# Rows of x turned between product tiles, and two low quarters on VectorE, in a graph + attention + expert layer on one core

## The chip, the cores and the metric

One core of a Trainium2 chip runs the whole layer as one program of 25298 instructions. The metric is the device time of one execution in microseconds. Before the change three runs gave 1471.56, 1474.73 and 1475.39 us, median 1474.73 us.

## What is computed

The reference takes x (1250 rows of 1024), 20000 edges (src, dst) sorted by dst, and the weights of three sublayers. Cut to what matters here:

```python
xn = layernorm(x)
# graph sublayer: count matrix of the edges (+ identity), degrees, then
h   = xn @ W.T + b
out = segment_sum(deg_inv_sqrt[row] * deg_inv_sqrt[col] * h[col], row)
x = x + graph(xn) + attention_with_random_features(xn)
x = x + top2_of_8_experts(layernorm(x))
```

The change touches only the first part: turning xn, the product `xn @ W.T`, and the edge count matrix.

## The kernel before

Rows are padded to 1280 and cut in TT = 10 blocks of 128. Three things are made in the first 290 us.

1. xn. ScalarE and GpSimd normalise the ten row blocks. TensorE transposes each block in two halves of four 128x128 pieces (L1633; index i = 0 to 19, block t = i // 2) into a PSUM bank. ScalarE copies the bank, rounded, to `xh` (L935), VectorE subtracts that from the bank and writes the rest to `xl` (L1199). The banks are 3 to 6 in turn. This is one loop on each engine, and TensorE then waits for all twenty halves (`xt_low` at 2 * TT) ahead of the first product tile.

2. The count matrix, in ten graph blocks of 128 rows. For each block VectorE makes one-hot matrices of its edges: a 128x128 one (L1192) and a 128x1280 one (L1193), called one one-hot below; there are 188 in all, in a ring of four buffers. TensorE multiplies each pair in three matmuls (L1616) into banks 0 to 2 (even blocks) or 3 to 5 (odd blocks), between an opening (L1609, L1611) and a closing (L1621). ScalarE's `keep_block(b)` squares what was left of the block before (L910), then copies the banks twice (L922, L923). GpSimd's `degrees(b)` adds the copy to the degrees (L689), makes the rests of it (L691) and stores them by a DMA from its own queue (L693). Blocks 0 to 9 need 52, 24, 20, 16, 16, 12, 12, 12, 12 and 12 one-hots.

3. The product h, in 40 tiles (i = TT * q + t) of 24 matmuls, by four quarters of the weight columns. For each of a quarter's eight slabs ScalarE rounds a raw slab to `wqh` (L906, `high_quarter`), and the rest of it goes to `wql` (L683, `low_quarter`). There are four raw buffers; SyncE loads the next slab when `w_ready` says that the low part of the slab four back was made. A tile ends in bank 6 or 7 and ScalarE copies it out (L956); TensorE may be at most two tiles ahead of that.

Each engine works strictly in its written order. TensorE does graph block 0, the twenty turns, and then tiles 0 to 39 with graph blocks 1 to 9 put in before tiles 3, 7, 10, 14, 17, 21, 24, 28 and 31 (`BREAKS`). ScalarE follows the same order, with `high_quarter(1)` right behind the turns and `high_quarter(2)` and `(3)` ahead of the copy of tiles 11 and 22. VectorE does one_hots(0), the twenty lows, then one_hots(1) to (9), as far ahead as the four buffers allow. GpSimd does low_quarter(0), degrees(0), low_quarter(1), degrees(1), (2), low_quarter(2), degrees(3) to (5), low_quarter(3), degrees(6) to (9). The graph product, the attention, the output projection and the experts follow; they hang on these results and are untouched.

Of the kernel before, what the change touches and what calls it, by code (L numbers as in the profile page):

```python
# [8 lines left out]
P = 128  # L9
N, D = 1250, 1024  # L10
TT = -(-N // P)
NP = TT * P
LAST = N - (TT - 1) * P
KT = D // P
# [24 lines left out]
BREAKS = (3, 7, 10, 14, 17, 21, 24, 28, 31)  # L39
DEG_AT = 33  # L40
REST_AT = 35

RING = 6
START = 5
# [3 lines left out]
ALU = mybir.AluOpType  # L48
# [11 lines left out]
def gps_layer(nc, x, dst_pairs, src_cols, dst_cols, wg, bg, wq, bq, wk, bk, wv, bv, wo, bo, orf,  # L60
# [6 lines left out]
    with ctx:  # L67
# [131 lines left out]

        def counts(b):  # L200
            return ATf[:, b + 1, :] if b < TT - 1 else last_raw

        def xn_tile(t):
            return xn_low[:, t, :] if t < TT // 2 else xn_high[:, t - TT // 2, :]
# [75 lines left out]
        def bank(b, n=CW):  # L280
            return PB[:, 512 * b:512 * b + n]
# [348 lines left out]
        def _(pool):  # L630
# [48 lines left out]
            def low_quarter(q):  # L679
                for k in range(KT):  # L680
                    i = KT * q + k
                    pool.wait_ge(w_high, i + 1)
                    g.tensor_tensor(wql[q % 2][:, k, :], raw_g[:, i % 4, :], wqh[q % 2][:, k, :].bitcast(F32),  # L683
                                    ALU.subtract).then_inc(w_ready, 1)

            def degrees(b):
                pool.wait_ge(at_evac, b + 3)
                pool.wait_ge(s_pchain, b + 1)
                g.tensor_tensor(degacc[:, :], degacc[:, :], counts(b), ALU.add).then_inc(s_pchain, 1)  # L689
                pool.wait_ge(s_pchain, b + 2)  # L690
                g.tensor_tensor(counts(b).bitcast(F32R), counts(b), AT[:, b, :].bitcast(F32), ALU.subtract).then_inc(rest_made, 1)  # L691
                pool.wait_ge(rest_made, b + 1)
                g.dma_start(rests[b], counts(b).bitcast(F32R)).then_inc(rest_stored, 16)  # L693
                if b == 0:
                    g.dma_start(rests[TT][:, 0:P], counts(0)[:, 0:P].bitcast(F32R)).then_inc(rest_stored, 16)
# [3 lines left out]
            low_quarter(1)  # L699
            for b in range(1, 3):  # L700
                degrees(b)
            low_quarter(2)
            for b in range(3, 6):
                degrees(b)
            low_quarter(3)
            for b in range(6, TT):
                degrees(b)
            pool.wait_ge(s_degcol, TT)
            g.tensor_tensor(dis[:, :], deg[:, :], mhalf[:, :], ALU.pow).then_inc(s_dis, 1)
# [177 lines left out]
        def _(act):  # L887
# [12 lines left out]
            def high_quarter(q):  # L900
                for k in range(KT):
                    i = KT * q + k
                    act.wait_ge(raw_in[i % 4], 16 * (i // 4 + 1))
                    if q >= 2:
                        act.wait_ge(tile_done, TT * (q - 1))
                    a.activation(wqh[q % 2][:, k, :], raw_g[:, i % 4, :], ACT.Copy).then_inc(w_high, 1)  # L906
# [5 lines left out]
            def keep_block(b):  # L912
                act.wait_ge(at_done, b + 1)
                if b >= 1:
                    rest_squares(b - 1)
                    act.wait_ge(rest_sum, b)
                    act.wait_ge(rest_stored, 16 * (b + 1))
                if b == TT - 2:

                    act.wait_ge(w_ready, NQ * KT)  # L920
                of = PB[:, 1536 * (b % 2):1536 * (b % 2) + NP]
                a.activation(AT[:, b, :], of, ACT.Copy)  # L922
                a.activation(counts(b), of, ACT.Copy).then_inc(at_evac, 1)  # L923

            def high_scaled(q):
                for b in range(TT):
                    act.wait_ge(h_bias, TT * max(q - 1, 0) + b + 1)
                    a.mul(hh[:, q % 2, b, :], hrf[:, q % 2, b, :], dis[:, b:b + 1]).then_inc(h_hi, 1)

            high_quarter(0)  # L930
            keep_block(0)
            for i in range(2 * TT):
                t, k0 = i // 2, 4 * (i % 2)
                act.wait_ge(xt_done, i + 1)
                a.activation(xh[:, k0:k0 + 4, t * P:(t + 1) * P],  # L935
                             bank(3 + i % 4).rearrange("p (k n) -> p k n", k=4), ACT.Copy).then_inc(xt_high, 1)
            high_quarter(1)
            for i in range(TILES):
                q, t = i // TT, i % TT
                if i in BREAKS:  # L940
                    keep_block(BREAKS.index(i) + 1)
                if i in (11, 22):
                    high_quarter(2 + i // 22)
                if i == REST_AT:
                    rest_squares(TT - 1)
                if i == TILES - 1:
                    act.wait_ge(s_dis, 1)
                    high_scaled(0)
                act.wait_ge(tile_done, i + 1)
                if i < SPILL:  # L950
                    to = hrf[:, q, t, :]
                else:
                    to = spill[:, i % 2, :]
                    if i >= SPILL + 2:
                        act.wait_ge(h_stored[i % 2], 16 * ((i - SPILL) // 2))
                a.activation(to, bank(7 - i % 2, QW), ACT.Copy).then_inc(tile_evac, 1)  # L956
# [181 lines left out]
        def _(dve):  # L1138
# [44 lines left out]
            def one_hots(b):  # L1183
                first = dve.value_load(rngi[0:1, 0, b:b + 1], min_val=0, max_val=PAIRS - 2)
                count = dve.value_load(rngi[0:1, 1, b:b + 1], min_val=1, max_val=PAIRS // 2)
                begin = dve.value_load(rngi[0:1, 3, b:b + 1], min_val=0, max_val=PAIRS * TT)
                with dve.Fori(0, count) as i:
                    at = nc.s_assert_within(first + 2 * i, 0, PAIRS - 2, skip_runtime_bounds_check_because="the last pair that a block needs is below PAIRS - 1")
                    for p in range(4):
                        col = 2 * at + p  # L1190
                        dve.wait_ge(oh_free, 4 * (begin + i) + p + 1)
                        v.tensor_scalar(ohd[:, p, :], iota[:, b * P:(b + 1) * P], dc[:, ds(col, 1)], None, ALU.is_equal)  # L1192
                        v.tensor_scalar(ohs[:, p, :], iota[:, :], sc[:, ds(col, 1)], None, ALU.is_equal).then_inc(oh_ready, 1)  # L1193

            one_hots(0)
            for i in range(2 * TT):
                t, k0 = i // 2, 4 * (i % 2)
                dve.wait_ge(xt_high, i + 1)
                v.tensor_tensor(xl[:, k0:k0 + 4, t * P:(t + 1) * P], bank(3 + i % 4).rearrange("p (k n) -> p k n", k=4),  # L1199
                                xh[:, k0:k0 + 4, t * P:(t + 1) * P].bitcast(F32), ALU.subtract).then_inc(xt_low, 1)  # L1200
            for b in range(1, TT):
                one_hots(b)

            def low_scaled(q, b):
                dve.wait_ge(h_hi, TT * q + b + 1)
# [388 lines left out]
        def _(pe):  # L1594
# [7 lines left out]
            def graph_block(b):  # L1602
# [19 lines left out]
                             start=False, stop=True, skip_group_check=True)  # L1622
                ins.then_inc(at_done, 1)

            graph_block(0)
            for i in range(2 * TT):
                t = i // 2
                pe.wait_ge(s_xn, t + 1)
                if i >= 4:
                    pe.wait_ge(xt_low, i - 3)  # L1630
                for q in range(4):
                    k = 4 * (i % 2) + q
                    ins = nc.tensor.transpose(bank(3 + i % 4)[:, q * P:(q + 1) * P], xn_tile(t)[:, k * P:(k + 1) * P], ident[:, :])  # L1633
                ins.then_inc(xt_done, 1)
            pe.wait_ge(xt_low, 2 * TT)
            for i in range(TILES):
                q, t = i // TT, i % TT
                if i in BREAKS:
                    graph_block(BREAKS.index(i) + 1)
                if i == DEG_AT:  # L1640
                    pe.wait_ge(s_pchain, TT + 1)
                    pe.wait_ge(at_evac, TT + 1)
                    for c0, n in CHUNKS:
                        ins = mm(PB[:, c0:c0 + n], ones[:, :], degacc[:, c0:c0 + n], start=True, stop=True)
                    ins.then_inc(s_deg, 1)
                if i == REST_AT + 1:
                    pe.wait_ge(rest_sum, TT)
                    mm(bank(3, TT)[0:1, :], ones[:, 0:1], lsum[:, :], start=True, stop=True).then_inc(s_deg, 1)
                if i >= 2:
                    pe.wait_ge(tile_evac, i - 1)  # L1650
                for k in range(KT):
                    pe.wait_ge(w_ready, KT * q + k + 1)
                    at = slice(t * P, (t + 1) * P)
                    o = bank(7 - i % 2, QW)
                    mm(o, xh[:, k, at], wqh[q % 2][:, k, :], start=(k == 0), stop=False)  # L1655
                    mm(o, xh[:, k, at], wql[q % 2][:, k, :], start=False, stop=False)  # L1656
                    ins = mm(o, xl[:, k, at], wqh[q % 2][:, k, :], start=False, stop=(k == KT - 1))  # L1657
                ins.then_inc(tile_done, 1)
# [341 lines left out]
```

## Time and profile before

| | us |
|---|---|
| median of three runs | 1474.73 |
| the profiled execution, its own time | 1479.25 |
| its span, first to last instruction | 1477.70 |
| TensorE busy in the span | 1367.7 |
| VectorE busy | 789.1 |
| ScalarE busy | 561.8 |
| GpSimd busy | 428.5 |

All rows below are of one profiled execution. In a timeline a row is: start in us, length in us, engine, source line, operation, output<-inputs, shapes, count, and in brackets the idle time of the engine before it with what ended it. Lines that follow each other may be merged in a row with a count above one; the length is then that of the group. PE is TensorE, PEld its weight load, DVE VectorE, ACT ScalarE, POOL GpSimd. A chain row is start, length, and the piece of work or the wait on the path that ended last.

### The profile page before, as it was taken

How to read it: one execution, taken by the hardware profiler on the slowest of the kernel's cores; microseconds unless marked ns; L12 is line 12 of the kernel's file. 1: busy time of each engine (PE TensorE's matmuls, PEld its weight loads, DVE VectorE, ACT ScalarE, POOL GpSimd, SP SyncE). 2: the span in 40 equal slices, each digit the busy share in tenths (PEclk: the TensorE clock that was granted, in tenths of full speed). 3: DMA queues.
4: the chain of work that ended last, by engine and by line, in shares of the span. 5: the costliest groups of instructions: out<-in, count | busy, mean ns of one | idle time of the engine just before them, and what ended most of it. 6: DMA issues, size and time to landing. Idle time of an engine off the chain costs nothing.

```text
span 1477.7 us, 25298 instructions
## 1 busy us (share of the span) xinstructions
PE 1367.7 (93%) x8199; PEld 1206.9 (82%) x8234; DVE 789.1 (53%) x1633; ACT 561.8 (38%) x957; POOL 428.5 (29%) x429
## 2 busy tenths in 40 slices
PE   5799989999999999999999999979999399999996
PEld 1476667999989999999999999967888387778785
DVE  7856554436256565656565656564454634444541
ACT  7422222402045454545454545421222223444441
POOL 7432453253420101010101010045032533333332
PEclk9999999999989999999999999968999599999998
DMA  4110111264310000000000000013245356766843
GB/s 164 49 46 24 60 65 61 78 195 137 97 44 15 29 14 28 14 28 14 28 14 28 14 28 0 0 57 101 73 174 190 119 173 202 208 205 213 285 128 55
DMA packets 58101, 127.78 MB, mean 86 GB/s; under 512 B 7626, under 2 KB 28826, under 8 KB 58048
## 3 DMA queue, kind: packets, MB, share of 16 engines
q1 hardware_dynamic: 48016, 96.79, 19.0%
q0 software_dynamic: 10032, 30.30, 8.6%
q8 instruction: 31, 0.51, 0.1%
q14 instruction: 22, 0.18, 0.0%
HBM read 91.46 MB, written 37.43 MB: 87 GB/s over the span
## 4 chain that ended last, share of the span: by engine, by line
PE 71%; DVE 9%; DMA 7%; issue 6%; ACT 4%; SPq 1%; POOL 1%; DVEq 1%; POOLq 0%; ACTq 0%
PE PB L1710 7%; PE PB L1712 7%; PE PB L1711 7%; PE PB L1616 7%; PE PB L1748 5%; PE PB L1771 4%; PE PB L1925 4%; PE PB L1926 4%; PE PB L1928 3%; DMA ebb<-expert_b 3%; PE PB L1695 2%; PE PB L1697 2%; PE PB L1696 2%; PE PB L1655 2%; PE PB L1657 2%
## 5 line engine op out<-in xcount | busy, mean ns | idle before, releaser
L1710 PE MATMUL PB<-xh,hw 128*128 128x416 f32 (+1 forms) x576 | 204.4, 355 | 0.0
L1712 PE MATMUL PB<-xh,hw 128*128 128x416 f32 (+1 forms) x576 | 203.6, 353 | 0.0
L1711 PE MATMUL PB<-xl,hw 128*128 128x416 f32 (+1 forms) x576 | 203.5, 353 | 0.0
L1925 PE MATMUL PB<-mwh,mth 128*128 128x512 f32 x368 | 148.6, 404 | 4.2 <-DVE mwl L1574 3.6
L716 POOL CAST hw<-hraw 128x1024 fp32r<-128x1024 f32 x24 | 24.9, 1038 | 424.1 <-DVE qphi L1317 202.3
L1926 PE MATMUL PB<-mwl,mth 128*128 128x512 f32 x368 | 144.4, 392 | 0.0
L1616 PE MATMUL PB<-ohs,ohd 128*128 128x512 bf16 (+1 forms) x530 | 112.6, 352 | 17.7 <-DVE ohs L1193 15.4
L1193 DVE TENSOR_SCALAR ohs<-iota,sc 128x1280 bf16<-128x1280 f16 x188 | 115.6, 615 | 0.0
L1928 PE MATMUL PB<-mwh,mtl 128*128 128x512 f32 x368 | 114.3, 392 | 0.0
L1616 PEld LDWEIGHTS PB<-ohs,ohd 128*128 128x128 bf16 x564 | 47.3, 100 | 81.5 <-DVE ohs L1193 47.9
L1710 PEld LDWEIGHTS PB<-xh,hw 128*128 128x128 f32 x576 | 109.1, 189 | 1.3
L1711 PEld LDWEIGHTS PB<-xl,hw 128*128 128x128 f32 x576 | 109.0, 189 | 1.3
L1712 PEld LDWEIGHTS PB<-xh,hw 128*128 128x128 f32 x576 | 108.8, 189 | 1.2
L1192 DVE TENSOR_SCALAR ohd<-iota,dc 128x128 bf16<-128x128 f16 x188 | 54.5, 290 | 90.0 <-PE PB L1616 85.9
L1683 PE MATMUL PB<-hh,AT 128*128 128x256 f32 x400 | 98.3, 287 | 3.3 <-DVE hr L1206 3.0
L1684 PE MATMUL PB<-hr,AT 128*128 128x256 f32 x400 | 97.5, 285 | 0.0
L1655 PE MATMUL PB<-wqh,xh 128*128 128x256 f32 x320 | 91.7, 287 | 3.2 <-DVE xl L1199 1.7
L1656 PE MATMUL PB<-wql,xh 128*128 128x256 f32 x320 | 90.5, 283 | 0.0
L1657 PE MATMUL PB<-wqh,xl 128*128 128x256 f32 x320 | 90.5, 283 | 0.0
L1027 ACT ACTIVATE qphi<-PB 128x416 f32<-128x416 f32 (+1 forms) x96 | 48.4, 513 | 104.8 <-PE PB L1761 93.5
L1771 PEld LDWEIGHTS PB<-kvs,qphi 128*128 128x128 f32 x640 | 83.4, 209 | 2.0 <-issue 1.9
L1925 PEld LDWEIGHTS PB<-mwh,mth 128*128 128x128 f32 x368 | 69.4, 189 | 18.7 <-issue 5.2
(295 smaller groups left out, 3090.3 us busy)
## 6 DMA issues: line engine op xcount, KB each, us to landing
mraw<-expert_w SPq DMA_DIRECT2D x64, 512.0 KB
count_rests<-ATf POOLq DMA_DIRECT2D x9, 640.0 KB, 3.5
xrow<-x SPq DMA_DIRECT2D x40, 128.0 KB, 3.0
y_scratch<-xrow SPq DMA_DIRECT2D x40, 128.0 KB, 1.9
yrow<-y_scratch SPq DMA_DIRECT2D x20, 256.0 KB, 2.8
x2n_half<-xhat SPq DMA_DIRECT2D x20, 256.0 KB, 2.3
out<-x SPq DMA_DIRECT2D x9, 512.0 KB
ATf<-wg SPq DMA_DIRECT2D x32, 128.0 KB, 2.2
```

The costliest lines, as they stand in the source:

```text
L1193: v.tensor_scalar(ohs[:, p, :], iota[:, :], sc[:, ds(col, 1)], None, ALU.is_equal).then_inc(oh_ready, 1)
L1616: ins = mm(PB[:, 1536 * s + c0:1536 * s + c0 + n], ohd[:, p, :], ohs[:, p, c0:c0 + n], start=False, stop=False, skip_group_check=True)
L1655: mm(o, xh[:, k, at], wqh[q % 2][:, k, :], start=(k == 0), stop=False)
L1657: ins = mm(o, xl[:, k, at], wqh[q % 2][:, k, :], start=False, stop=(k == KT - 1))
L1683: mm(o, AT[:, b, at], hh[:, q % 2, b, :], start=(b == 0), stop=False)
L1710: mm(bank(i, n), hw[:, wi, 0, k, :], xh[:, k, c0:c0 + n], start=(k == 0), stop=False)
L1711: mm(bank(i, n), hw[:, wi, 0, k, :], xl[:, k, c0:c0 + n], start=False, stop=False)
L1712: ins = mm(bank(i, n), hw[:, wi, 1, k, :], xh[:, k, c0:c0 + n], start=False, stop=(k == KT - 1))
L1771: ins = mm(bank(6 + f % 2)[:, q * (DK + 1):(q + 1) * (DK + 1)], qphi[:, m, t * P:(t + 1) * P], kvs[:, h, m, :], start=(m == 0), stop=(m == ...
L1925: mm(y[c], mth[:, k, :], mwh[par][:, k, c * CW:(c + 1) * CW], start=(k == 0), stop=False)
L1926: mm(y[c], mth[:, k, :], mwl[par][:, k, c * CW:(c + 1) * CW], start=False, stop=False)
L1928: ins = mm(y[c], mtl[:, k, :], mwh[par][:, k, c * CW:(c + 1) * CW], start=False, stop=(k == KT - 1))
```

## The change

Turns. A new table `TURNS` puts the turning of row blocks 0 and 1 ahead of tile 0, block 2 ahead of tile 1, blocks 3 and 4 ahead of tile 2, block 5 ahead of tile 4, 6 ahead of tile 5, 7 and 8 ahead of tile 6, and 9 ahead of tile 8. `TURN_BLOCK` says behind which graph block each is turned. The turns use three banks, the ones that the graph blocks don't hold then (3 to 5, then 0 to 2, then 3 to 5), and each half waits for the low part three halves back. Tile t waits only for the lows of its own row block. Turns 5 to 8 wait for the squares of graph block 0 (`rest_sum`), turn 9 for those of block 1. VectorE makes one_hots(0), lows 0 to 4, one_hots(1), lows 5 to 8, one_hots(2), low 9, one_hots(3) and so on. `high_quarter(1)` moves to just ahead of `keep_block(1)`.

Quarters. `low_quarter(2)` and `(3)` leave GpSimd; VectorE makes them, behind one_hots(3) and one_hots(6).

```diff
--- before.py
+++ after.py
@@ -39,6 +39,8 @@
 BREAKS = (3, 7, 10, 14, 17, 21, 24, 28, 31)
 DEG_AT = 33
 REST_AT = 35
+TURNS = ((0, 1), (2,), (3, 4), (), (5,), (6,), (7, 8), (), (9,))
+TURN_BLOCK = (0, 0, 0, 0, 0, 1, 1, 1, 1, 2)
 
 RING = 6
 START = 5
@@ -200,6 +202,9 @@
         def counts(b):
             return ATf[:, b + 1, :] if b < TT - 1 else last_raw
 
+        def turn_bank(i):
+            return bank(3 * ((TURN_BLOCK[i // 2] + 1) % 2) + i % 3)
+
         def xn_tile(t):
             return xn_low[:, t, :] if t < TT // 2 else xn_high[:, t - TT // 2, :]
 
@@ -699,11 +704,7 @@
             low_quarter(1)
             for b in range(1, 3):
                 degrees(b)
-            low_quarter(2)
-            for b in range(3, 6):
-                degrees(b)
-            low_quarter(3)
-            for b in range(6, TT):
+            for b in range(3, TT):
                 degrees(b)
             pool.wait_ge(s_degcol, TT)
             g.tensor_tensor(dis[:, :], deg[:, :], mhalf[:, :], ALU.pow).then_inc(s_dis, 1)
@@ -927,18 +928,24 @@
                     act.wait_ge(h_bias, TT * max(q - 1, 0) + b + 1)
                     a.mul(hh[:, q % 2, b, :], hrf[:, q % 2, b, :], dis[:, b:b + 1]).then_inc(h_hi, 1)
 
+            def high_turned(t):
+                for i in (2 * t, 2 * t + 1):
+                    k0 = 4 * (i % 2)
+                    act.wait_ge(xt_done, i + 1)
+                    a.activation(xh[:, k0:k0 + 4, t * P:(t + 1) * P],
+                                 turn_bank(i).rearrange("p (k n) -> p k n", k=4), ACT.Copy).then_inc(xt_high, 1)
+
             high_quarter(0)
             keep_block(0)
-            for i in range(2 * TT):
-                t, k0 = i // 2, 4 * (i % 2)
-                act.wait_ge(xt_done, i + 1)
-                a.activation(xh[:, k0:k0 + 4, t * P:(t + 1) * P],
-                             bank(3 + i % 4).rearrange("p (k n) -> p k n", k=4), ACT.Copy).then_inc(xt_high, 1)
-            high_quarter(1)
             for i in range(TILES):
                 q, t = i // TT, i % TT
+                if i == BREAKS[0]:
+                    high_quarter(1)
                 if i in BREAKS:
                     keep_block(BREAKS.index(i) + 1)
+                if i < len(TURNS):
+                    for turned in TURNS[i]:
+                        high_turned(turned)
                 if i in (11, 22):
                     high_quarter(2 + i // 22)
                 if i == REST_AT:
@@ -1192,14 +1199,28 @@
                         v.tensor_scalar(ohd[:, p, :], iota[:, b * P:(b + 1) * P], dc[:, ds(col, 1)], None, ALU.is_equal)
                         v.tensor_scalar(ohs[:, p, :], iota[:, :], sc[:, ds(col, 1)], None, ALU.is_equal).then_inc(oh_ready, 1)
 
-            one_hots(0)
-            for i in range(2 * TT):
-                t, k0 = i // 2, 4 * (i % 2)
-                dve.wait_ge(xt_high, i + 1)
-                v.tensor_tensor(xl[:, k0:k0 + 4, t * P:(t + 1) * P], bank(3 + i % 4).rearrange("p (k n) -> p k n", k=4),
-                                xh[:, k0:k0 + 4, t * P:(t + 1) * P].bitcast(F32), ALU.subtract).then_inc(xt_low, 1)
-            for b in range(1, TT):
+            def low_turned(t):
+                for i in (2 * t, 2 * t + 1):
+                    k0 = 4 * (i % 2)
+                    dve.wait_ge(xt_high, i + 1)
+                    v.tensor_tensor(xl[:, k0:k0 + 4, t * P:(t + 1) * P], turn_bank(i).rearrange("p (k n) -> p k n", k=4),
+                                    xh[:, k0:k0 + 4, t * P:(t + 1) * P].bitcast(F32), ALU.subtract).then_inc(xt_low, 1)
+
+            def low_quarter(q):
+                for k in range(KT):
+                    i = KT * q + k
+                    dve.wait_ge(w_high, i + 1)
+                    dve.wait_ge(w_ready, i)
+                    v.tensor_tensor(wql[q % 2][:, k, :], raw_g[:, i % 4, :], wqh[q % 2][:, k, :].bitcast(F32),
+                                    ALU.subtract).then_inc(w_ready, 1)
+
+            for b in range(TT):
                 one_hots(b)
+                for t in range(TT):
+                    if TURN_BLOCK[t] == b:
+                        low_turned(t)
+                if b in (3, 6):
+                    low_quarter(1 + b // 3)
 
             def low_scaled(q, b):
                 dve.wait_ge(h_hi, TT * q + b + 1)
@@ -1622,21 +1643,32 @@
                              start=False, stop=True, skip_group_check=True)
                 ins.then_inc(at_done, 1)
 
+            def turn_rows(t):
+                pe.wait_ge(s_xn, t + 1)
+                b = TURN_BLOCK[t]
+                if b:
+                    pe.wait_ge(rest_sum, b)
+                for i in (2 * t, 2 * t + 1):
+                    if i >= 3:
+                        pe.wait_ge(xt_low, i - 2)
+                    for q in range(4):
+                        k = 4 * (i % 2) + q
+                        ins = nc.tensor.transpose(turn_bank(i)[:, q * P:(q + 1) * P], xn_tile(t)[:, k * P:(k + 1) * P], ident[:, :])
+                    ins.then_inc(xt_done, 1)
+
             graph_block(0)
-            for i in range(2 * TT):
-                t = i // 2
-                pe.wait_ge(s_xn, t + 1)
-                if i >= 4:
-                    pe.wait_ge(xt_low, i - 3)
-                for q in range(4):
-                    k = 4 * (i % 2) + q
-                    ins = nc.tensor.transpose(bank(3 + i % 4)[:, q * P:(q + 1) * P], xn_tile(t)[:, k * P:(k + 1) * P], ident[:, :])
-                ins.then_inc(xt_done, 1)
-            pe.wait_ge(xt_low, 2 * TT)
             for i in range(TILES):
                 q, t = i // TT, i % TT
                 if i in BREAKS:
-                    graph_block(BREAKS.index(i) + 1)
+                    b = BREAKS.index(i) + 1
+                    if b <= 2:
+                        pe.wait_ge(xt_low, 2 * TURN_BLOCK.index(b))
+                    graph_block(b)
+                if i < len(TURNS):
+                    for turned in TURNS[i]:
+                        turn_rows(turned)
+                if i < TT:
+                    pe.wait_ge(xt_low, 2 * (t + 1))
                 if i == DEG_AT:
                     pe.wait_ge(s_pchain, TT + 1)
                     pe.wait_ge(at_evac, TT + 1)
```

## Rows read from the trace of the kernel before

**Rows 1.** the page: the chain that ended last, share of the span by engine

```profile
PE 71%; DVE 9%; DMA 7%; issue 6%; ACT 4%; SPq 1%; POOL 1%; DVEq 1%; POOLq 0%; ACTq 0%
```

**Rows 2.** timeline of PE, the turns and the first tile

```profile
58.31 1.94 PE L1633 MATMUL PB<-ident,xn_low 128*128 128x128 f32 x16
62.21 4.64 PE L1633 MATMUL PB<-ident,xn_low 128*128 128x128 f32 x24 [1.96 <-DVE xl L1199]
...
74.30 0.39 PE L1655 MATMUL PB<-wqh,xh 128*128 128x256 f32 x1 [1.67 <-DVE xl L1199]
```

**Rows 3.** timeline of DVE, the first six lows of the turned halves

```profile
61.37 3.73 DVE L1199 TENSOR_TENSOR xl<-PB,xh 128x512 fp32r<-128x512 f32 x6 [3.75 <-ACT xh L935]
```

**Rows 4.** timeline of PE, openings (L1609) and closings (L1621) of graph blocks

```profile
83.04 0.71 PE L1609 MATMUL PB<-iota,zero 128*128 128x512 f16 x3
...
97.81 0.22 PE L1621 MATMUL PB<-iota,zero 128*128 128x2 f16 x3
...
121.74 0.22 PE L1621 MATMUL PB<-iota,zero 128*128 128x2 f16 x3
140.29 0.22 PE L1621 MATMUL PB<-iota,zero 128*128 128x2 f16 x3
...
165.16 0.22 PE L1621 MATMUL PB<-iota,zero 128*128 128x2 f16 x3
...
200.16 0.22 PE L1621 MATMUL PB<-iota,zero 128*128 128x2 f16 x3
...
224.05 0.22 PE L1621 MATMUL PB<-iota,zero 128*128 128x2 f16 x3
```

**Rows 5.** timeline of DVE, one-hots of blocks 0, 1 and 7

```profile
41.09 0.70 DVE L1192 TENSOR_SCALAR ohd<-iota,dc 128x128 bf16<-128x128 f16 x1
...
48.16 0.24 DVE L1192 TENSOR_SCALAR ohd<-iota,dc 128x128 bf16<-128x128 f16 x1
...
75.63 0.26 DVE L1192 TENSOR_SCALAR ohd<-iota,dc 128x128 bf16<-128x128 f16 x1 [1.39 <-issue]
...
84.61 0.26 DVE L1192 TENSOR_SCALAR ohd<-iota,dc 128x128 bf16<-128x128 f16 x1 [3.86 <-PE PB L1616]
...
85.23 0.25 DVE L1192 TENSOR_SCALAR ohd<-iota,dc 128x128 bf16<-128x128 f16 x1
...
211.78 3.21 DVE L1193 TENSOR_SCALAR ohs<-iota,sc 128x1280 bf16<-128x1280 f16 x1
```

**Rows 6.** timeline of POOL, a low quarter, degrees of blocks 0 and 6, a later split

```profile
40.79 3.25 POOL L683 TENSOR_TENSOR wql<-ATf,wqh 128x256 fp32r<-128x256 f32 x4
...
60.93 2.91 POOL L689 TENSOR_TENSOR degacc<-degacc,ATf 128x1280 f32<-128x1280 f32 x1 [13.20 <-ACT ATf L923]
...
211.77 2.88 POOL L689 TENSOR_TENSOR degacc<-degacc,ATf 128x1280 f32<-128x1280 f32 x1
214.73 3.01 POOL L691 TENSOR_TENSOR ATf<-ATf,AT 128x1280 fp32r<-128x1280 f32 x1
...
334.45 2.46 POOL L718 TENSOR_TENSOR hw<-hraw,hw 128x1024 fp32r<-128x1024 f32 x1
```

**Rows 7.** timeline of ACT behind graph block 3, and the quarter's last slab

```profile
143.08 1.24 ACT L923 ACTIVATE ATf<-PB 128x1280 f32<-128x1280 f32 x1
...
144.46 1.35 ACT L906 ACTIVATE wqh<-ATf 128x256 fp32r<-128x256 f32 x4
147.84 0.42 ACT L906 ACTIVATE wqh<-ATf 128x256 fp32r<-128x256 f32 x1 [2.04 <-DMA ATf<-wg]
```

**Rows 8.** the chain that ended last, behind graph block 3

```profile
150.78 0.39 PE PB L1655
```

**Rows 9.** timeline of DVE, an operation with both inputs in SBUF

```profile
335.23 1.97 DVE L1206 SCALAR_TENSOR_TENSOR hr<-hrf,dis,hh 128x256 fp32r<-128x256 f32 x1 [0.58 <-ACT hh L928]
```

**Rows 10.** busy time by stretch; behind the engines' sums PEclk, DMA share and GB/s

```profile
64.00:66.00 2.00, 2.00 (x11) 2.00 (x10) 1.80 (x3) 1.49 (x3) 2.00 (x1) 0.50 0.00 0
...
218.00:220.00 2.00, 1.70 (x5) 0.74 (x6) 2.00 (x7) 0.00 (x0) 0.57 (x1) 0.50 0.48 179
```

## The prediction

> **What bounds the kernel now.** I read the chain that ended last first: TensorE is 71% of it [rows 1]. Then I read TensorE's timeline over the first 290 us, for the change touches nothing later, and whatever it moves at graph block 9 shifts the rest as a whole. That stretch has two kinds of work. Product tiles are bound by TensorE: three take 83.04 - 74.30 us, so 2.9 us each [rows 2, 4]. Graph blocks are bound by VectorE: one-hots start every 85.23 - 84.61 = 0.62 us [rows 5], four of them are ready when a block opens, and VectorE gets its next free buffer 84.61 - 83.04 = 1.6 us behind the opening. So a block of n one-hots lasts 1.6 + 0.62 (n - 4) + 0.7 us. That gives 14.7 for block 1 (measured 97.81 - 83.04 = 14.8 [rows 4]) and 9.8 for the 16 of block 3 (measured 140.29 - 121.74, less three tiles, 9.9). The turns take 74.30 - 58.31 = 16.0 us, though TensorE needs about 0.11 us for each of 80 transposes (sixteen in 1.94 us, the modelled end of the last included) [rows 2]: copy and low of a half set the pace, six lows in 3.73 us, 0.62 each [rows 3]. Last I asked what else disturbs these stretches, and found GpSimd.
>
> **GpSimd and VectorE hold each other up.** While GpSimd makes eight low slabs, from 40.79 on, five one-hots take 48.16 - 41.09 = 7.1 us in place of 3.1: 3.9 us lost [rows 5, 6]. In block 7 a one-hot that started at 211.78 took 3.21 us, just beyond the end of GpSimd's 2.88 us addition that began at 211.77; GpSimd's next one was in turn 3.01 us [rows 5, 6]. It isn't special to one-hots: a VectorE operation with both inputs in SBUF, started at 335.23 inside GpSimd's 334.45 to 336.91, took 1.97 us and ended 0.3 us behind it [rows 6, 9]. The lows of the turns read one input from PSUM, and kept 0.62 us each while GpSimd made the degrees of block 0 from 60.93 on [rows 3, 6].
>
> The Trainium skill (SBUF — State Buffer, section Who interferes with whom) says that a VectorE instruction with two SBUF inputs contends with a GpSimd one that reads SBUF, that the later one blocks fully, and that VectorE with one SBUF input outside its two-port modes does not. The rows agree. By it the moved low quarters, two SBUF inputs each, aren't free beside `degrees`; without it one would take rival B's time below.
>
> **The change part by part.** All of it is reckoned by the time at which graph blocks close [rows 4].
>
> Part 1, to the close of block 1. Block 0 ends at 58.3 as before. The first three halves are turned at once, the fourth waits for the first low, as the old fifth did until 62.21 [rows 2]. The second low ends at about 62.7, and tile 0 starts at 62.9. TensorE ran at half clock (0.50 at 64 to 66 us) behind the same 2 us of idling [rows 10]; over about 3.4 us that costs 1.7. Tile 0 ends at 67.5; block 2 (0.9) and tile 1 bring 71.3; blocks 3 and 4 need 1.8 plus about 0.5 for a bank, for with three banks the fourth half waits for the first's copy and low; tile 2 ends at 76.5. The last low ends at 75.0. one_hots(1) can't run ahead any more: it starts 1.39 us later, the same issue time as before [rows 5], at 76.4. low_quarter(1) now follows the copy of tile 2, at 77.5, so its eight subtractions fall on one_hots(1), bound by VectorE, and not on tiles. I take the 3.9 us of block 0. Close: 76.4 + 24 x 0.62 + 3.9 + 0.7 = 96.0, against 97.8: -1.8. Bounds of the held time: 2.6 us (the four one-hots of 75.63 beside the old low_quarter(1)) and 4; without the clock's fall -3.5.
>
> Part 2, to the close of block 2. Four tiles 11.6, four turned row blocks 3.6, one bank wait 0.5. The squares (`rest_sum`) end 1.5 us behind a block's close, while tile 3 runs, so that wait costs nothing while a tile is in front of it. The last low ends 14.4 behind the close of block 1, one_hots(2) starts at 15.8, and ends at 15.8 + 12.5 + 0.7 = 29.0. Before: 121.74 - 97.81 = 23.9. +5.1.
>
> Part 3, to the close of block 3. One row block is turned (0.9). low 9 ends 6.1 behind the close, one_hots(3) starts at 7.5, inside degrees(2): two additions of 2.9 from 4.0 to 9.9. It is held till 9.9, and 16 one-hots and the tail end at 20.6. Before 18.55. +2.1 (0.9 if not held).
>
> Part 4, to the close of block 4. GpSimd no longer has low_quarter(2) in front of degrees(3), so degrees(3) starts as soon as the copy is there, 4.1 us behind the close (143.08 + 1.24 = 144.3 before) [rows 7]. ScalarE rounds the first slab at 144.46 on the same clock, so VectorE's first subtraction comes half a microsecond later and finds GpSimd at work. I expect it held to the first addition's end (7.1), the second held to the second's end (10.5), the third and fourth right behind. Each frees a raw buffer, and the next slab lands 2.2 us later (old row: the first of the second four was rounded at 147.84, having waited for its DMA [rows 7]; SyncE is queued behind `w_ready`). The fifth to eighth slab are thus rounded until 13.8. ScalarE holds the copy of tile 11 for all that time and tile 13 needs its bank. Before, that wait ended at 150.78, 10.5 behind the close [rows 8]; now at 14.2. The idle 5.5 us should again bring half clock for about 4 us (as 0.50 at 218 to 220 [rows 10]): 2.1. Then tile 13 and an undisturbed block: 14.2 + 2.9 + 2.1 + 9.8 = 29.0, against 165.16 - 140.29 = 24.9. +4.2, though the old block 4 lost 1.6 to degrees(3) and this one doesn't. Not held, it would be 9.1 + 2.9 + 9.9 = 21.9: -3.0.
>
> Part 5, block 7. The same chain: subtractions end 14.3 behind the close of block 6, then 1.4 to issue, 12 one-hots and the tail: 15.7 + 7.5 + 0.7 = 23.9, with half clock in its first 4 us about 25.0. Before 224.05 - 200.16 = 23.9, for that block was held up by degrees(6) (the 3.21 us one-hot) and low on clock itself. +1.1; not held 18.8: -5.1. Here three tiles end at 8.7, so only the opening waits.
>
> Free, for one reason: copies `rest_squares`, `keep_block` and `high_quarter(1)` on ScalarE, which sits idle through blocks; the raw loads on SyncE's queue, which have 2.9 us tiles in front of them; and degrees(1) and (2), which end before GpSimd is asked again. If a DMA of a raw slab is late, tile 13's wait grows by it. Behind block 7 the order of work is as before.
>
> Sum: -1.8 + 5.1 + 2.1 + 4.2 + 1.1 = +10.7 us, from a span of 1477.7 to 1488.4. The profiled execution took 1479.25, 4.5 above the median of three; I carry the difference over to the median: 1474.73 + 10.7 = 1485.4.
>
> **Rivals.**
> A (forecast), 1485.4. For it: the three held operations of rows 5, 6 and 9.
> B, the moved subtractions aren't held: parts 4 and 5 become -3.0 and -5.1, the sum -2.7, 1472.0: not slower than before. It needs VectorE to get the SBUF port between or ahead of GpSimd's additions. Parts 1 to 3 lose 5.4 us, and parts 4 and 5 gain 8.1 if nothing is held, so the sign turns where the holds cost 2.7 us instead of the 13.4 of A. Against it: the 1.97 us row.
> C, the clock doesn't fall behind the idles: less 1.7, 2.1 and 1.0, so +5.9, 1480.6. For it: tile 13 waited 1.7 us before with the clock full. Against: the new idle is longer.
> D, B holds and low_quarter(1) doesn't disturb block 1 either (-3.9 more): 1468.1. That is the change doing all it can; the 7.1 us row speaks against it.
> E, worse: later DMAs and held `one_hots`, with a longer half clock in parts 2 to 4, 4 to 5 us above A: 1490.
>
> **How the numbers follow.** A 0.54, B 0.14, C 0.14, D 0.07, E 0.11. A measurement can tell 0.3%, 4.4 us. Faster (below 1470.3): D and a third of B, 0.12. Same (to 1479.2): the rest of B, a third of C and a little of A, 0.20. Slower: 0.68. The range 1472 to 1490 reaches from B's time to E's; it leaves out D, half of B and half of E, about 0.2. A and C alone would be 1480 to 1488.
>
> **What would show it.** Part 1: tile 0 near 63 in place of 74.3, block 1 closing near 96 with one-hots 1.6 us apart while L683 runs. Part 2: L1616 of block 2 paced by VectorE from its first. Part 3: one long L1192 at the start of one_hots(3). Part 4: L683's work now on VectorE, two of its eight subtractions 2 to 3 us long, and a TensorE idle of 5 us ahead of tile 13. Part 5: block 7 as long as before though degrees(6) is off it. I am wrong if those subtractions are all 0.4 us (B), or if block 1 keeps its 14.8 us.

## The result, and the profile after

The changed kernel takes 1489.82 us (median of four runs, 1488.75 to 1491.78) against 1474.36 us for the kernel before, whose median is now one of four runs: a ratio of 1.0102, with a 95% interval of 1.0078 to 1.0126. It is 15.5 us slower. The forecast was 10.7 us slower. The profiled execution spans 1490.2 us. Ratios here and below leave out two executions in a slower state, one at 2713 us among the twelve of v3_turns_halves_busy and one at 1562 us among those of the kernel before.

First the timeline of TensorE (PE) in the changed kernel, from which the closings of the graph blocks are read. L1656 is a transpose, L1630 opens a block, L1642 closes it, L1637 multiplies the one-hots, L1687 is the first matmul of a slab of a tile. These lines answer to [rows 2, 4].

```profile
58.29 1.51 PE L1656 MATMUL PB<-ident,xn_low 128*128 128x128 f32 x12
62.10 0.66 PE L1656 MATMUL PB<-ident,xn_low 128*128 128x128 f32 x4 [2.30 <-DVE xl L1206]
...
76.31 0.72 PE L1630 MATMUL PB<-iota,zero 128*128 128x512 f16 x3
...
96.16 0.22 PE L1642 MATMUL PB<-iota,zero 128*128 128x2 f16 x3
...
125.56 0.22 PE L1642 MATMUL PB<-iota,zero 128*128 128x2 f16 x3
...
146.17 0.22 PE L1642 MATMUL PB<-iota,zero 128*128 128x2 f16 x3
...
162.18 0.58 PE L1687 MATMUL PB<-wqh,xh 128*128 128x256 f32 x1 [7.06 <-ACT hrf L963]
166.59 0.72 PE L1630 MATMUL PB<-iota,zero 128*128 128x512 f16 x3
...
176.37 0.22 PE L1642 MATMUL PB<-iota,zero 128*128 128x2 f16 x3
...
211.37 0.22 PE L1642 MATMUL PB<-iota,zero 128*128 128x2 f16 x3
220.16 0.71 PE L1630 MATMUL PB<-iota,zero 128*128 128x512 f16 x3
...
231.03 7.85 PE L1637 MATMUL PB<-ohs,ohd 128*128 128x512 bf16 x33 [10.11 <-DVE ohs L1200]
238.72 0.22 PE L1642 MATMUL PB<-iota,zero 128*128 128x2 f16 x3
```

Set against [rows 4], the whole difference builds up in five steps. In the table the first row has the times of the close, in us from the start of the span; each row below has the time from one close to the next.

| interval | before | after | difference | forecast |
|---|---|---|---|---|
| to the close of block 1 | 97.81 | 96.16 | -1.7 | -1.8 |
| block 1 to 2 | 23.9 | 29.4 | +5.5 | +5.1 |
| block 2 to 3 | 18.6 | 20.6 | +2.1 | +2.1 |
| block 3 to 4 | 24.9 | 30.2 | +5.3 | +4.2 |
| block 6 to 7 | 23.9 | 27.4 | +3.5 | +1.1 |

That is +14.7 us. Blocks 5, 6, 8 and 9 close at the old distances within 0.02 us. The two profiled spans differ by 12.5 us only, since what follows block 9, the same work in both, took 2.2 us less in the changed kernel's execution. In the twelve profiled executions of this document that last part took 1211.9 to 1223.7 us. So single spans and times are too coarse for terms of a few us, and the closings are read instead.

The two new waits of TensorE, 7.06 and 10.11 us, stand in those lines. The chain that ended last shows what lies behind the first of them: start, length, piece of work, in us.

```profile
150.07 0.39 ACT hrf L963
150.46 0.31 ACT wqh L907
150.79 2.73 DVE wql L1214
153.62 2.97 DVE wql L1214
156.68 0.44 DVE wql L1214
157.13 3.93 DMA ATf<-wg
161.08 0.42 ACT wqh L907
161.53 0.44 DVE wql L1214
```

Beside it stands the timeline of GpSimd (POOL) in the same stretch:

```profile
150.27 2.95 POOL L694 TENSOR_TENSOR degacc<-degacc,ATf 128x1280 f32<-128x1280 f32 x1 [13.75 <-ACT ATf L924]
153.30 2.99 POOL L696 TENSOR_TENSOR ATf<-ATf,AT 128x1280 fp32r<-128x1280 f32 x1
156.59 0.56 POOL L698 DMA_DIRECT2D count_rests<-ATf  x1 [0.30 <-POOL ATf L696]
```

Two subtractions of 128x256 took 2.73 and 2.97 us and ended 0.3 us behind GpSimd's two operations; the third took 0.44. VectorE had become the engine on which SyncE's loads, ScalarE's copy of tile 11 and so TensorE's tile 13 hang.

The load behind it took 3.93 us from the freeing of its buffer to its landing. In the kernel before, the chain has the same step at this place with 2.19 us:

```profile
147.83 2.19 DMA ATf<-wg
```

Busy time by stretch (us, then busy time and count of PE, PEld, DVE, ACT, POOL, then the granted clock, DMA share, GB/s) shows two more things:

```profile
158.00:160.00 2.00, 0.00 (x0) 0.00 (x0) 0.59 (x2) 0.42 (x1) 0.00 (x0) 0.66 1.05 380
160.00:162.00 2.00, 0.00 (x0) 0.00 (x0) 0.43 (x1) 0.92 (x3) 0.00 (x0) 0.50 0.77 260
```

The DMA engines were full, with the 640 KB store that GpSimd issued at 156.59. And TensorE's clock went to 0.50, which is the lower of its two levels, 1.2 GHz, behind the idling.

The start of one_hots(3) shows the same kind of hold on a one-hot, and the low ahead of it, with one input in PSUM, was untouched at 1.29 us for two. Timeline of VectorE (DVE):

```profile
130.38 1.29 DVE L1206 TENSOR_TENSOR xl<-PB,xh 128x512 fp32r<-128x512 f32 x2 [5.42 <-ACT xh L935]
133.20 2.50 DVE L1199 TENSOR_SCALAR ohd<-iota,dc 128x128 bf16<-128x128 f16 x1 [1.53 <-issue]
```

### The profile page after: what moved, and what is told of

It is laid out like the page before. It is cut to its first block, busy times and chain, and to the rows that moved or that the text cites. A ratio compares the mean times of both kernels' runs of the same rounds, so it can differ in the third digit from the quotient of the medians.

```text
span 1490.2 us, 25307 instructions
## 1 busy us (share of the span) xinstructions
PE 1368.8 (92%) x8199; PEld 1206.7 (81%) x8234; DVE 802.8 (54%) x1649; ACT 560.8 (38%) x957; POOL 426.0 (29%) x413
## 4 chain that ended last, share of the span: by engine, by line
PE 74%; DVE 8%; issue 5%; ACT 4%; DMA 4%; DVEq 1%; POOL 1%; SPq 1%; POOLq 0%; ACTq 0%
PE PB L1637 7%; PE PB L1742 7%; PE PB L1743 7%; PE PB L1744 7%; PE PB L1780 5%; PE PB L1957 4%; PE PB L1958 4%; PE PB L1960 4%; PE PB L1803 4%; PE PB L1727 3%; PE PB L1728 2%; PE PB L1729 2%; PE PB L1715 2%; PE PB L1716 2%; DMA ebb<-expert_b 2%
## 5 line engine op out<-in xcount | busy, mean ns | idle before, releaser
L717 POOL CAST hw<-hraw 128x1024 fp32r<-128x1024 f32 x24 | 24.9, 1039 | 428.7 <-DVE qphi L1338 206.8
L1637 PE MATMUL PB<-ohs,ohd 128*128 128x512 bf16 (+1 forms) x530 | 113.7, 350 | 26.2 <-DVE ohs L1200 23.7
L1637 PEld LDWEIGHTS PB<-ohs,ohd 128*128 128x128 bf16 x564 | 45.5, 99 | 92.9 <-DVE ohs L1200 61.5
L1200 DVE TENSOR_SCALAR ohs<-iota,sc 128x1280 bf16<-128x1280 f16 x188 | 104.2, 554 | 0.0
L1687 PE MATMUL PB<-wqh,xh 128*128 128x256 f32 x320 | 93.6, 293 | 7.1 <-ACT hrf L963 7.1
L1199 DVE TENSOR_SCALAR ohd<-iota,dc 128x128 bf16<-128x128 f16 x188 | 61.9, 329 | 52.0 <-PE PB L1637 40.3
L1018 ACT ACTIVATE kphi<-PB 128x512 f32<-128x512 f32 x80 | 46.3, 596 | 105.5 <-PE PB L1780 56.3
L1780 PEld LDWEIGHTS PB<-vt,kphi 128*128 128x128 f32 (+1 forms) x640 | 80.1, 204 | 6.4 <-DVE vt L1347 5.5
```

The source lines that it names most:

```text
L1637: ins = mm(PB[:, 1536 * s + c0:1536 * s + c0 + n], ohd[:, p, :], ohs[:, p, c0:c0 + n], start=False, stop=False, skip_group_check=True)
L1780: ins = mm(bank(5)[:, m * (DK + 1):(m + 1) * (DK + 1)], kphi[0:n, t, m * P:(m + 1) * P], vt[0:n, t, h, :], start=(t == 0), stop=(t == TT - 1))
```

## The experiments

All are read in the same way: the distance from the close of block 0 to those of later blocks, in one profiled execution each. In the table "1 to 3" is from the close of block 0 to that of block 3. The ratio is to the kernel before, timed on the same chip. The clocked times are of the whole layer, and their intervals are 7 to 10 us wide, so they tell the direction of an edit, and the closings its size.

| kernel | 1 to 3 | block 4 | block 7 | all, to block 9 | ratio, interval |
|---|---|---|---|---|---|
| before | 82.1 | 24.9 | 23.9 | 200.8 | |
| changed | 88.0 | 30.2 | 27.4 | 215.5 | 1.0102, 1.0078 to 1.0126 |
| e1_turns_only | 87.8 | 24.9 | 22.7 | 205.4 | 1.0047, 1.0022 to 1.0072 |
| e2_quarters_only | 82.1 | 31.1 | 27.9 | 211.1 | 1.0080, 1.0046 to 1.0114 |
| e3_store_later | 88.6 | 29.5 | 26.7 | 214.7 | 1.0101, 1.0073 to 1.0129 |
| e5_degrees_later | 88.0 | 28.1 | 25.0 | 211.0 | 1.0070, 1.0039 to 1.0101 |
| e4_keep_busy | 86.4 | 31.0 | 27.6 | 215.0 | 1.0068, 1.0040 to 1.0096 |
| e6_q1_earlier | 83.1 | 30.2 | 27.4 | 210.7 | 1.0055, 1.0033 to 1.0078 |
| v1_halves | 81.2 | 21.5 | 19.9 | 192.6 | 0.9931, 0.9905 to 0.9957 |
| v2_halves_busy | 81.2 | 21.5 | 18.7 | 191.4 | 0.9926, 0.9900 to 0.9951 |
| v2_again | 81.3 | 21.5 | 18.7 | 191.4 | 0.9922, 0.9897 to 0.9946 |
| v3_turns_halves_busy | 83.1 | 21.5 | 19.9 | 194.4 | 0.9949, 0.9924 to 0.9974 |

### One half of the change at a time

e1_turns_only is the changed kernel with the quarters back on GpSimd:

```diff
-            for b in range(3, TT):
+            low_quarter(2)
+            for b in range(3, 6):
                 degrees(b)
+            low_quarter(3)
+            for b in range(6, TT):
+                degrees(b)
...
-                if b in (3, 6):
-                    low_quarter(1 + b // 3)
```

> Only the turns are moved; low quarters 2 and 3 stay on GpSimd as before. If the changed kernel's loss splits as its trace reads (closes of blocks 1, 2 and 3 at -1.7, +5.5 and +2.1 us against before, and +5.3 and +3.5 in blocks 4 and 7), this one is 5.9 us slower than before, and its blocks 4 and 7 close 24.9 and 23.9 us behind blocks 3 and 6, as before. Rival: the turns are harmless and the whole loss comes from the quarters; then it equals before. A second rival is that the turns push the degrees later and so change blocks 4 and 7 too; then those two intervals differ from 24.9 and 23.9.

Blocks 1 to 3 took 87.8 us instead of 82.1, and block 4 its old 24.9. Block 7 took 22.7, 1.2 less than before, which the second rival had named as a sign that the turns reach it. The trace doesn't bear that out: two one-hots are held there as before (3.22 and 2.87 us), and what differs is TensorE's granted clock. It was between 0.50 and 0.65 from 216 to 224 us in the kernel before, and 0.66, 0.50 and 0.99 in the three 2 us stretches from 222 us on in this one. The kernel is slower than before by 3 to 11 us, as its interval has it; the closings say 4.6.

e2_quarters_only is the kernel before, with GpSimd's two calls taken out, `low_quarter` defined on VectorE as in the changed kernel, and this behind one_hots(3) and one_hots(6):

```diff
             for b in range(1, TT):
                 one_hots(b)
+                if b in (3, 6):
+                    low_quarter(1 + b // 3)
```

> Only low quarters 2 and 3 are moved to VectorE; all turns stand ahead of the first tile as before. If the subtractions held by GpSimd's additions and the late raw slabs are the cause, this is 5.3 + 3.5 = 8.8 us slower than before, with the close of block 3 at the old 140.3 and blocks 4 and 7 at 30.2 and 27.4 us. Rival: the loss in blocks 4 and 7 needs the turns in front of it; then this is within 2 us of before.

Block 3 closed at 140.34, as before, and blocks 4 and 7 took 31.1 and 27.9 us. So the quarters lose 10.2 us by themselves. The two halves lose 4.6 + 10.2 = 14.8 us apart and 14.7 together. The totals add, but not each part: in the two quarters' blocks e2 loses 1.4 us more than the changed kernel, and e1's block 7 is 1.2 us shorter than before. These two nearly cancel, and that is luck.

### What holds the subtractions

e5_degrees_later, from the changed kernel, moves GpSimd's work out of the way of the subtractions:

```diff
                 pool.wait_ge(at_evac, b + 3)
+                if b in (3, 6):
+                    pool.wait_ge(w_ready, KT * (2 + b // 3))
```

> The changed kernel, but GpSimd's degrees of blocks 3 and 6 wait until VectorE has made the whole low quarter. If GpSimd's additions hold the subtractions, all sixteen subtractions now take 0.42 us, the last ends near 9 us behind the close of block 3 and 6 instead of 16.7, and tile 13 hardly waits. The additions then fall on the next one-hots, which take the hold: block 4 closes about 24.4 us behind block 3 (30.2 in the changed kernel, 24.9 before), block 7 about 23 behind block 6 (27.4 and 23.9). Sum: about 5 us slower than before, 10 faster than the changed kernel. Rival: the subtractions were late for another reason (their own latency, the loads); then they stay late and this is no faster than the changed kernel.

The line's summary gives shortest, median and longest duration in ns. First the changed kernel, then this one:

```profile
L1214 DVE TENSOR_TENSOR wql<-ATf,wqh x16: 424/426/2962, 150.8 to 227.3; 128x256 fp32r<-128x256 f32 x16
```

```profile
L1216 DVE TENSOR_TENSOR wql<-ATf,wqh x16: 424/425/426, 150.8 to 218.8; 128x256 fp32r<-128x256 f32 x16
```

All sixteen took 0.42 us once GpSimd's additions were later. The last one began at 155.88, 9.7 us behind the close of block 3, and tile 13 waited 0.91 us. The edit moves GpSimd's store along with its additions, but e3 below moves the store alone and the hold stays. So it is shown that the additions hold the subtractions. The sum was too hopeful: 28.1 and 25.0 us instead of 24.4 and 23, so 4.5 us less than the changed kernel where 10 were expected. The additions fell on the one-hots, and held two of them (0.25 us each otherwise). First VectorE's, then TensorE's timeline of this kernel:

```profile
158.22 1.23 DVE L1201 TENSOR_SCALAR ohd<-iota,dc 128x128 bf16<-128x128 f16 x1 [1.91 <-issue]
...
159.83 2.87 DVE L1201 TENSOR_SCALAR ohd<-iota,dc 128x128 bf16<-128x128 f16 x1
```

```profile
159.96 0.71 PE L1639 MATMUL PB<-ohs,ohd 128*128 128x512 bf16 x3
163.21 11.11 PE L1639 MATMUL PB<-ohs,ohd 128*128 128x512 bf16 x44 [2.54 <-DVE ohs L1202]
```

The changed kernel's block 4 does the same 44 recorded matmuls in 9.12 us. Here the granted clock was 0.59 at 162 to 164 us and 0.50 from 164 to 168. Block 4 opened 7.6 us sooner behind the close of block 3 than in the changed kernel, and lasted 5.4 us longer.

### The store in front of the raw slabs

e3_store_later, from the changed kernel:

```diff
                 pool.wait_ge(rest_made, b + 1)
+                if b in (3, 6):
+                    pool.wait_ge(w_high, KT * (2 + b // 3))
                 g.dma_start(rests[b], ...)
```

> The changed kernel, but GpSimd starts the 640 KB store of the rests of blocks 3 and 6 only when ScalarE has rounded the whole quarter. Theory 1: two of the slabs were late since that store was in front of them on the DMA engines (the last slab was rounded 15.7 us behind the close of block 3 instead of the 13.8 forecast). Then the last slab comes about 2 us sooner in both places, and the kernel is 3 to 4 us faster than the changed one, some 11.5 us slower than before; the two held subtractions stay near 3 us. Theory 2: the late slabs come from SyncE's queue or the holds alone; then nothing changes, 15 us slower than before.

The held subtractions stayed (five in 7.37 us, as before the edit). The last slab was rounded at 161.01, 14.1 us behind the close of block 3 instead of about 15.3, and blocks 4 and 7 shrank by 0.7 us each. The clocked time does not show it. Theory 1 has the mechanism right and the size wrong: the store costs 1.4 us in both blocks together, not 3 to 4.

### The turns

e4_keep_busy puts ten matmuls of zeros into an unread bank ahead of the fourth half's wait:

```diff
                 for i in (2 * t, 2 * t + 1):
+                    if i == 3:
+                        for _ in range(10):
+                            mm(bank(6), zero[:, :], iota[:, 0:512], start=True, stop=True, skip_group_check=True)
                     if i >= 3:
                         pe.wait_ge(xt_low, i - 2)
```

> The changed kernel with ten matmuls of zeros into bank 6, which nobody reads, while TensorE would wait for the first low ahead of the fourth half. If the half clock that follows that 2.3 us of idling is what makes tile 0 last 4.5 us, tile 0 now lasts 2.9 us, block 1 closes 1.5 us earlier (94.7) and the whole is 13.5 instead of 15 us slower than before. Rival: tile 0 is slow for another reason (it waits for its weights or lows); then it stays at 4.5 us and block 1 at 96.2.

The same stretch by its busy time, first in the changed kernel, then here (columns as above; the clock is the first of the last three numbers):

```profile
64.00:66.00 2.00, 2.00 (x12) 2.00 (x11) 0.12 (x1) 0.00 (x0) 2.00 (x1) 0.50 0.00 0
```

```profile
64.00:66.00 2.00, 2.00 (x19) 2.00 (x19) 0.00 (x0) 0.30 (x1) 2.00 (x1) 1.00 0.03 8
```

12 matmuls against 19 in 2 us: what made tile 0 slow was the clock. Block 1 closed 36.4 us behind block 0 instead of 38.0. That the zero matmuls kept the clock isn't shown by this run alone, for in e6 below it stayed up without them, behind the same 2.30 us of idling. Taken over all profiled executions, the clock fell in this place in six of eight without them, and in none of the four with them (e4, v2, v2_again, v3). That points to the zeros, but four are few. The timed gain against the changed kernel isn't clear of their intervals.

e6_q1_earlier, from the changed kernel, takes low_quarter(1) off the one-hots:

```diff
-                if i == BREAKS[0]:
-                    high_quarter(1)
...
+                if i in (1, 2):
+                    high_quarter(1, 4 * (i - 1), 4 * i)
```

with `high_quarter(q, k0, k1)` going over those slabs only.

> The changed kernel, but ScalarE rounds quarter 1 in two halves, ahead of the copies of tiles 1 and 2, so that GpSimd makes its low parts beside tiles instead of beside one_hots(1). If these subtractions slow the one-hots of block 1 (0.62 to 1.6 us apart in the changed kernel between 77 and 84 us), block 1 now closes about 3 us earlier, near 93, and the whole is 12 us slower than before. Rival: block 1 is late only since VectorE starts it late; then it closes at 96 as before.

Block 1 closed 33.0 us behind block 0 instead of 38.0, so 4.9 us earlier; 3 were expected. In this execution the clock was at 1.00 from 62 to 68 us, which is some 1.5 of the 4.9. The opening of block 1 came just that much earlier. From its opening to its close the block took 3.4 us less: that is the hold of GpSimd's eight subtractions on one-hots. One hold was left, the first one-hot's, which took 0.5 us longer than the next; with it the two make the 3.9 us of the prediction:

```profile
74.76 1.02 DVE L1200 TENSOR_SCALAR ohs<-iota,sc 128x1280 bf16<-128x1280 f16 x1
75.70 0.24 DVE L1199 TENSOR_SCALAR ohd<-iota,dc 128x128 bf16<-128x128 f16 x1
```

### A version that beats both

If holds and waits for loads are the matter, the cure is to keep the quarters on GpSimd and never put eight slabs in one gap. v1_halves, from the kernel before:

```diff
+HALVES = (11, 18, 22, 25)
...
-            low_quarter(2)
-            for b in range(3, 6):
+            low_quarter(2, 0, 4)
+            for b in range(3, 5):
                 degrees(b)
-            low_quarter(3)
-            for b in range(6, TT):
+            low_quarter(2, 4, 8)
+            for b in range(5, 6):
+                degrees(b)
+            low_quarter(3, 0, 4)
+            for b in range(6, 7):
+                degrees(b)
+            low_quarter(3, 4, 8)
+            for b in range(7, TT):
                 degrees(b)
...
-                if i in (11, 22):
-                    high_quarter(2 + i // 22)
+                if i in HALVES:
+                    at = HALVES.index(i)
+                    high_quarter(2 + at // 2, 4 * (at % 2), 4 * (at % 2) + 4)
```

> The kernel before, with quarters 2 and 3 rounded and lowered in halves of four slabs (ahead of the copies of tiles 11, 18, 22 and 25) by ScalarE and GpSimd, so that no slab waits for a load and never eight low parts and the degrees lie in one gap. Block 4 should close 21.6 us behind block 3 (24.9 before: no wait of tile 13, no held one-hot), block 7 18.8 behind block 6 (23.9 before; 2.7 of hold are left), the others as before: 8 us faster than before. Rival: GpSimd's four subtractions and degrees still end behind the opening of blocks 5 and 8 as well, and hold one-hots there; then those gaps grow from 18.9 and the gain is 4 us or less.

Block 4 took 21.5 us and block 7 19.9: 3.4 and 4.0 us less than before. Blocks 5 and 8 kept their distances, so the rival falls. It is 6 to 14 us faster than before by its interval. The halves take away two things at once, the wait of tile 13 behind a load and most of the hold, and no run tells them apart. What is left of the hold in block 7 stands in its timeline, first GpSimd's rests of block 6, then a one-hot:

```profile
207.09 2.89 POOL L692 TENSOR_TENSOR ATf<-ATf,AT 128x1280 fp32r<-128x1280 f32 x1
```

```profile
207.15 3.18 DVE L1201 TENSOR_SCALAR ohs<-iota,sc 128x1280 bf16<-128x1280 f16 x1
```

v2_halves_busy adds to it, in the loop of the turns:

```diff
+                if i == 4:
+                    for _ in range(10):
+                        mm(bank(7), zero[:, :], iota[:, 0:512], start=True, stop=True, skip_group_check=True)
                 if i >= 4:
                     pe.wait_ge(xt_low, i - 3)
```

> v1_halves with ten matmuls of zeros into bank 7 while TensorE would wait for the first low in the turns. Before, the turns' transposes ran at half clock from 62.9 to 66.4 and five halves came 0.85 us apart instead of 0.6. If the clock is kept the turns end 1.2 us earlier and the whole is 9 us faster than before. Rival: copies and lows bound the turns anyway; then it equals v1_halves.

> v2_halves_busy once more, as the partner of the next kernel on the same chip: 8 to 9 us faster than before; the first three graph blocks behind block 0 close 81.2 us behind it.

Blocks 1 to 3 took 81.2 us in v1 and in v2 alike. The clock didn't fall there in v1's profiled execution, so the zero matmuls had nothing to save; whether they save anything over many runs stays open. Block 7 took 18.7 instead of 19.9. The hold in it is the same (3.18 us in both), and no zeros stand there; the clock fell in v1 and not in v2, and why is not shown. Busy time by stretch, first in v1, then in v2:

```profile
212.00:214.00 2.00, 2.00 (x8) 0.77 (x6) 2.00 (x7) 0.00 (x0) 0.00 (x0) 0.50 0.68 248
```

```profile
212.00:214.00 2.00, 2.00 (x11) 0.71 (x10) 1.43 (x5) 0.00 (x0) 0.00 (x0) 1.00 0.01 0
```

v3_turns_halves_busy is the changed kernel with e6's, e4's and v1's edits together, so with the turns between tiles and most of what disturbed them taken away.

> The turns of the changed kernel with all that disturbed them taken away: quarter 1 rounded and lowered beside tiles 1 and 2, zero matmuls that keep the clock, and quarters 2 and 3 in halves on GpSimd. If turning between tiles is by itself no gain (TensorE pays the 0.9 us of each row block, and one_hots of blocks 1 to 3 start without a lead, those of block 3 held by degrees(2)), blocks 1 to 3 close 81.5 us behind block 0, and the whole lies within 1 us of v2_again. Rival: the turns do save their 16 us once undisturbed; then blocks 1 to 3 close under 79 us and the whole is 2 us or more faster than v2_again.

Blocks 1 to 3 took 83.1 us, against 81.3 in v2_again, where 81.5 was expected. To the close of block 9 it is 3.0 us behind, where the expectation allowed 1; 1.2 of them are in block 7, where the clock fell to 0.50 again and in v2_again it didn't. The medians were 1469.63 and 1465.61 us, and the two intervals to the kernel before overlap. So the turns between tiles don't gain here; the trace has them 1.8 us behind. They aren't quite undisturbed: the first one-hot of block 3 is still held by degrees(2).

```profile
128.77 2.50 DVE L1211 TENSOR_SCALAR ohd<-iota,dc 128x128 bf16<-128x128 f16 x1 [1.54 <-issue]
```

The prediction puts that hold at 1.2 us (+2.1 or, not held, +0.9 in part 3). By this estimate the turns would still be some 0.6 us behind without it; no run has it taken away.

## Why the prediction was right, and where its sizes were off

Direction, range and mechanism held. The forecast was 1485.4 us and the measured time 1489.8, 0.2 us inside the upper end of the range. The mechanism is A's, both holds and the fallen clock. The number is E's (1490), and it came by only one of E's terms, the later DMAs; the held one_hots and the longer half clock of parts 2 to 4 did not come. That the total still lies inside the range is in part luck.

- Part 1 (-1.8): measured -1.7. Tile 0 began at 62.7, block 1's one-hots were up to 1.6 us apart from 77.4 to 84.4, and block 1 closed at 96.2. The two terms could be taken apart: 1.5 for the clock (e4, 1.7 forecast) and 3.4 for GpSimd's subtractions, with 0.5 more still left (e6, 3.9 forecast). Without either, in e6, the part was a gain of 6.5 us.
- Part 2 (+5.1): +5.5. one_hots(2) started 16.2 us behind the close instead of 15.8, mostly for its issue, which took 1.66 us instead of 1.39.
- Part 3 (+2.1): +2.1, with the one long L1199 that was asked for, 2.50 us.
- Part 4 (+4.2): +5.3. The two holds were as worked out (2.7 and 3.0 us, then 0.44). The term that failed is the load of the later slabs, 2.2 us each by the old row: the one on the chain took 3.93. The prediction let degrees(3) start earlier but forgot that its store moves with it, and it came in front of the loads. A step that is moved takes its DMA along. Tile 13 began 16.0 us behind the close, not 14.2, and lasted 4.4 us at the lower clock, not 5.0. e3 shows 0.7 us to be that store; the other 0.4 of the 1.1 isn't explained.
- Part 5 (+1.1): +3.5, so 2.4 more. The last subtraction ended 16.3 us behind the close of block 6 instead of 14.3, with a load of 3.96 us on the chain in front of it; 0.7 of these 2.0 is the store (e3), the rest isn't explained. The step from there to the first one-hot took 2.14 us and not 1.4: another 0.7. From the first one-hot to the close it took 8.9 us, 0.4 less than the 9.3 forecast, though the clock was at 0.50 from 224 to 232.
- "Free": the prediction put the raw loads at nothing, since tiles of 2.9 us stood in front of them. They were not free, as part 4 has it. No loss was found at the copies and squares.
- Rival B needed subtractions of 0.4 us; two of eight in each quarter took about 3. Rival C needed the clock to stay up: it fell to 0.50 at 64, at 160 and at 224 us. It names 1.7 us as the old wait of tile 13; the trace has 1.54, and nothing hangs on it. Rival D needed B and unhindered one-hots in block 1; both were held.

Two reasons make the turns a loss where 16 us seemed to be had. TensorE pays for each of the 80 transposes on its own path, where before they lay in the shadow of ScalarE and VectorE: block 2 opens 15.9 us behind the close of block 1 instead of 11.7. And one-hots, which before were four ahead, now start from nothing, since VectorE's written order puts the lows in front of them.

## What to carry to other kernels

Before handing work from GpSimd to VectorE, look at what GpSimd does in that stretch instead: beside its additions of 3 us, VectorE's subtractions with both inputs in SBUF waited until each addition had ended, and 0.42 us became 3. The one-hots, with one large input in SBUF, waited too; the lows with one input in PSUM did not. Filling a gap of one engine with work of another needs that each consumer's lead stays: here the ring of four one-hots was lost. Cutting the quarters in halves that fit the gaps gained 7.4 us in blocks 4 and 7; moving them to another engine lost 8.8. And a step that is moved takes its DMA along.

## What the runs showed of the hardware

- The hold ends with the instruction: operations of 0.42 us took 2.73 and 2.97 beside GpSimd additions of 2.95 and 2.99, and 0.42 to 0.43 without (e5). Between two such additions VectorE got one operation in. It goes both ways: four subtractions of GpSimd took 3.32 and 3.62 us beside the one-hots of block 1 in the changed kernel, and 2.82 with VectorE idle in v1_halves.
- TensorE's clock fell behind some idles of about 2 us and not behind others: it was 0.50 at 64 to 66 us behind 1.96 us before [rows 2, 10] and behind 2.30 after the change, and stayed at 1.00 behind 1.95 us in v1_halves and 2.30 in e6_q1_earlier. In all it fell in six of eight executions (before, changed, e1, e2, e3, e5). With ten matmuls of zeros in the gap it was at 1.00 in all four (e4, v2, v2_again, v3).
- A 128 KB load took 3.93 us instead of 2.19 while a 640 KB store of another queue filled the DMA engines (380 GB/s). With that store moved away (e3) the last slab came 1.2 us sooner.
